# Zero products in the pauses of the first groups, last-group weights spread by selecting products, and a one-instruction residual sum, in an audio tower kernel

## The reference, cut to what matters

```python
h = tok(x)                                   # 92 patches of 16 x 32 -> 128 features
h = h + attn(layernorm(h))                   # 8 heads of 64; softmax, heads mixed 8x8, norm over heads, times v
h = h + ffn(layernorm(h))
# ffn, for each token t (T = 64 * 92):
scores = softmax(xf @ gate_w.T); topk_w, topk_i = top_k(scores, 2); topk_w /= topk_w.sum(-1)
combine[t, topk_i] = topk_w                  # T x 8, two entries per row
eo = relu(xf @ w1[e] + b1[e]) @ w2[e] + b2[e]     # eight experts
y = sum_e combine[:, e] * eo[e];  out = y + relu(xf @ sw1 + sb1) @ sw2 + sb2
```

## Time and profile before

| | |
|---|---|
| median of 3 runs | 630.79 us (629.08 to 631.88) |
| the profiled execution | 634.0 us, of it a span of 632.2 us |
| PE busy | 604.8 us, 96% of the span |
| PEld, DVE, ACT, POOL busy | 527.6, 435.9, 406.5, 369.5 us |
| chain that ended last | PE 89%, DVE 3%, ACT 2%, POOL 2%, DMA 2%, issue 1% |
| granted TensorE clock | mean 0.973 of full speed |

### The profile page before, as it was taken

The page is one execution under the profiler, slowest core; times in us unless marked ns, Lnnn a source line. Parts: engine busy times, 40 slices in busy tenths (PEclk is TensorE's granted clock), DMA queues, the critical chain, the costliest instruction groups (busy, mean ns, idle before and its releaser), DMA issues.

```text
span 632.2 us, 17001 instructions
## 1 busy us (share of the span) xinstructions
PE 604.8 (96%) x6275; PEld 527.6 (83%) x6275; DVE 435.9 (69%) x1322; ACT 406.5 (64%) x1346; POOL 369.5 (58%) x545
## 2 busy tenths in 40 slices
PE   8887889999999999999999999999999999998895
PEld 7767789898989989898989888898988888887773
DVE  4453647778677777778777767777687767776543
ACT  3476657686867767676867667676857767676110
POOL 2754538585766748575756748575756747546100
PEclk9987869999999999999999999999999999999897
DMA  6000030120303030120302030120303020201112
GB/s 233 25 3 26 1 98 26 38 98 10 126 2 109 27 110 26 49 87 14 121 2 111 25 111 25 59 78 14 123 2 121 16 109 3 85 25 42 70 30 91
DMA packets 15459, 37.43 MB, mean 59 GB/s; under 512 B 1808, under 2 KB 4240, under 8 KB 15376
## 3 DMA queue, kind: packets, MB, share of 16 engines
q1 hardware_dynamic: 15376, 36.34, 16.9%
HBM read 33.13 MB, written 3.20 MB: 57 GB/s over the span
## 4 chain that ended last, share of the span: by engine, by line
PE 89%; DVE 3%; ACT 2%; POOL 2%; DMA 2%; issue 1%; SPq 0%; DVEq 0%; POOLq 0%; ACTq 0%
PE ps_fill L413 16%; PE ps_fill L414 14%; PE ps_fill L415 13%; PE ps_mix L641 12%; PE ps_dots L629 11%; PE ps_fill L777 7%; PE ps_av L649 7%; PE ps_fill L569 5%; PE ps_fill L769 2%; PE ps_fill L751 1%; DMA spread<-weights 1%; PE ps_fill L752 1%; PE ps_fill L741 1%; POOL sum L1226 1%; ACT sq L810 1%
## 5 line engine op out<-in xcount | busy, mean ns | idle before, releaser
L802 ACT ACTIVATE ex<-ps_dots,negmax 128x92 f32<-128x92 f32 x384 | 123.9, 334 | 31.3 <-DVE negmax L1069 31.2
L1226 POOL TENSOR_TENSOR sum<-sq 92x384 f32<-92x384 f32 x64 | 64.1, 1002 | 73.7 <-ACT sq L810 73.6
L1220 POOL TENSOR_TENSOR probs<-ex,rinv 128x552 f32<-128x552 f32 x64 | 71.1, 1112 | 57.9 <-DVE rinv L1075 57.9
L1166 DVE SCALAR_TENSOR_TENSOR act<-ps_fill,b_neg,spread 128x368 f32<-128x368 f32 x123 | 68.3, 594 | 28.4 <-PE ps_fill L415 21.7
L641 PEld LDWEIGHTS ps_mix<-mixk,probs 64*92 64x92 f32 x1536 | 69.5, 161 | 18.2 <-issue 10.6
L641 PE MATMUL ps_mix<-mixk,probs 64*92 64x64 f32 x1536 | 78.3, 250 | 3.1 <-DVE aT L1085 2.7
L629 PE MATMUL ps_dots<-xT,yT 128*64 128x92 f32 x1536 | 76.8, 250 | 4.0 <-ACT ex L802 4.0
L629 PEld LDWEIGHTS ps_dots<-xT,yT 128*64 128x64 f32 x1536 | 65.0, 139 | 15.5 <-ACT ex L802 8.3
L802 ACT ACTIVATION_READ_ACCUMULATOR ex<-ps_dots,negmax 128x1 f32 x384 | 77.7, 202 | 0.0
L1085 DVE TENSOR_TENSOR aT<-ps_mix,arstd 92x384 f32<-92x384 f32 x128 | 64.3, 542 | 7.2 <-ACT arstd L820 7.2
L810 ACT ACTIVATE sq<-ps_mix 92x768 f32<-92x768 f32 x64 | 51.6, 806 | 13.2 <-PE ps_mix L641 12.2
(11 more groups left out here) (190 smaller groups left out, 1524.0 us busy)
## 6 DMA issues: line engine op xcount, KB each, us to landing
spread<-weights SPq DMA_DIRECT2D x64, 368.0 KB, 5.3
xin<-in_x SPq DMA_DIRECT2D x16, 372.0 KB, 3.0
out<-fT SPq DMA_DIRECT2D x16, 184.0 KB, 1.9
act<-w_raw SPq DMA_DIRECT2D x1, 576.0 KB, 6.5
w_sb<-w_raw SPq DMA_DIRECT2D x1, 576.0 KB, 7.2
qkv<-qk_raw SPq DMA_DIRECT2D x1, 512.0 KB, 5.1
spread<-tok_raw SPq DMA_DIRECT2D x1, 256.0 KB, 3.8
spread<-wv_raw SPq DMA_DIRECT2D x1, 256.0 KB, 5.3
```

The costliest lines, as they stand in the source:

```text
L802: last = act.activation(ex[:, s % 2, c, :], ps_dots[:, c // HALF, o:o + N], ACT.Exp, bias=negmax[:, c:c + 1], accum_out=sums[:, s % 2, c:c ...
L1166: dve.scalar_tensor_tensor(out=act1[:, e, :], in0=ps[:, 0:W], scalar=b1_neg[:, e:e + 1], in1=spread[:, e, :], op0=ALU.max, op1=ALU.mult).t ...
L1220: pool.tensor_tensor(probs[:, s % 2, :, :], ex[:, s % 2, :, :], rinv[:, s % 2, :].unsqueeze(2).broadcast_to([128, CHUNKS, N]), ALU.mult).t ...
L1226: pool.tensor_tensor(sum4[:, :, :, :], sq[:, :, 0:4, :], sq[:, :, 4:8, :], ALU.add)\
```

## The change

**Still products.** `STILL` lists four places: before `dots 2` and `mix 2` of iteration 0 (4 and 9 products), before `dots 1` and `CT` of iteration 1 (17 and 23). There `still_products` waits until a shared bank is free and issues that many 128 x 368 products of the zero columns of `act1_split[0]` into it; the next user of the bank overwrites them. `ORDER_1` is the same list as `STEPS` and serves only the counting of bank uses. `FILL_BUSY`, empty, goes.

**Selecting products.** POOL builds `shares` in `prepG` (iteration 0): for each expert a 128 x 128 matrix with ones in rows e and 32 + e. All eight first products of the last group move to iteration 16, behind `RT` (`T0` to `T7`, ahead of `YF` and `CT`), in five PSUM places used in turn; ACT empties them as relu into `spread`. In iteration 17, once `combT` is there, `S0` to `S7` multiply `shares[e]` with `combT`, which gives expert e's weight on all partitions in PSUM, and DVE makes `act1 = (spread - b1) * ps`. The store and loads of the last group's weights (lines 891, 548, 552) go.

**Residual.** `shift` adds the bias to hT on POOL (one instruction for two), and `OP` is one DVE instruction of 368 columns for four.

```diff
@@ -95,6 +95,8 @@
 WIDE = tuple(f"T{e}" for e in range(E))
+SHARES = tuple(f"S{e}" for e in range(E))
+PLACES = 5
@@ -112,7 +114,7 @@
              (LAST - 2, "TX2"): 15, (LAST - 2, "RT"): 6}
-FILL_BUSY = {}
+STILL = {(0, ("dots", 2)): (4, "Y7"), (0, ("mix", 2)): (9, "Y7"), (1, ("dots", 1)): (17, "OP"), (1, "CT"): (23, "Y1")}
@@ -138,6 +140,15 @@
+ORDER_1 = [('mix', 0), ('sq', 0), ('dots', 0), ('max', 0), 'XE', ('av', 0), 'Z0', 'XO', ('exa', 0), 'Z2', ('rstd', 0), 'Z1',
...
+ ('ev', 3)]
@@ -147,14 +158,17 @@
  [('mix', 0), ('sq', 0), ('av', 0), ('ev', 0), 'Z0', ('rstd', 0), ('scale', 0), 'Z5', 'Z1', 'Z8', ('av', 1),
-  ('ev', 1), 'Z4', 'Z6', 'OP', 'Z2', 'TH2', 'Z7', 'NH2', 'Z3', 'TX2', 'RT', 'R2', 'R3', 'YF', 'CT', 'hold'],
- ['Z8', 'Z3', 'T6', 'Z0', 'Z1', 'T5', 'T2', 'T7', 'T4', 'YF']]
+  ('ev', 1), 'Z4', 'Z6', 'OP', 'Z2', 'TH2', 'Z7', 'NH2', 'Z3', 'TX2', 'RT', 'T0', 'T1', 'R2', 'T2', 'T3', 'T4', 'T5',
+  'T6', 'T7', 'R3', 'YF', 'hold', 'CT'],
+ ['Z8', 'S0', 'S1', 'S2', 'S3', 'S4', 'S5', 'S6', 'S7', 'YF']]
...
         return ORDER_0
+    if isinstance(G, int) and G == 1:
+        return ORDER_1
@@ -213,6 +227,10 @@
         filled_then = [other for other in ORDER_0[:ORDER_0.index(step)] if present(other, G)] + SETUP
+        return more + sum(BANK.get(other) == BANK[step] for other in filled_then)
+    if isinstance(G, int) and G == 1:
+        filled_then = [other for other in ORDER_0 if present(other, 0)] + SETUP
+        filled_then += [other for other in ORDER_1[:ORDER_1.index(step)] if present(other, 1)]
@@ -329,6 +346,7 @@
         flat = sb("flat", [E, W])
+        shares = sb("shares", [128, E, 128], F32R)
@@ -494,8 +514,10 @@
-            n = [other for other in order(LAST - 1) if other in WIDE].index(step)
-            return [ps_dots[:, 0, :], ps_dots[:, 1, :], ps_mix[:, 0, :], ps_mix[:, 1, :], ps_av[:, :]][n], n + 1
+            steps = order(LAST - 2) + order(LAST - 1)
+            n = [other for other in steps if other in WIDE + SHARES].index(step)
+            places = [ps_dots[:, 0, :], ps_dots[:, 1, :], ps_mix[:, 0, :], ps_mix[:, 1, :], ps_av[:, :]]
+            return places[n % PLACES], n + 1
@@ -542,7 +564,7 @@
                     load(G + 2)
-                if step == "CT":
+                if step == "CT" and exists(G + LAG[step] + 1, NG):
@@ -614,6 +636,14 @@
+            def still_products(step, G):
+                count, free = STILL[G, step]
+                wait_free(pe, free, G)
+                columns = act1_split[0][:, 0:4, :].rearrange("p e w -> p (e w)")
+                for _ in range(count):
+                    pe.matmul(bank(free)[:, 0:W], columns[:, 0:128], columns[:, 0:W], start=True, stop=True)
@@ -655,6 +685,8 @@
                 keep_busy(step, G)
+                if (G, step) in STILL:
+                    still_products(step, G)
@@ -672,7 +704,19 @@
                         pe.wait_ge(oT_ready, B)
+                        wait_emptied(pe, "TX2", G)
+                    at_least(pe, wide_emptied, n - PLACES)
                     products(to[:, 0:W], [w[:, int(step[1]), :] for w in w1_split], [m[:, 0:W] for m in x2T])\
+                        .then_inc(wide_filled, 1)
+                    return
+                if step in SHARES:
+                    to, n = wide(step)
+                    if n == E + 1:
+                        pe.wait_ge(shares_ready, 1)
+                        wait_emptied(pe, "CT", G - 1)
+                    pe.wait_ge(wide_emptied, min(n - PLACES, E))
+                    at_least(pe, wide_scaled, n - PLACES - E)
+                    pe.matmul(to[:, 0:W], shares[:, int(step[1]), :], combT[:, :], start=True, stop=True)\
@@ -693,11 +737,6 @@
                     pe.wait_ge(oT_ready, SLOTS * g + SLOTS)
-                if FILL_BUSY.get(step, 0) and 0 <= g and G < LAST - 2:
-                    wait_free(pe, step, G)
-                    columns = w1_split[0][:, 0:4, :].rearrange("p e w -> p (e w)")
-                    for _ in range(FILL_BUSY[step]):
-                        pe.matmul(bank(step)[:, 0:W], columns[:, 0:128], columns[:, 0:W], start=True, stop=True)
@@ -759,10 +798,10 @@
                     if direct(G):
-                        experts = [other for other in order(G) if other in EXPERTS + WIDE + (f"Z{E}",)]
+                        experts = [other for other in order(G) if other in EXPERTS + SHARES + (f"Z{E}",)]
                         for other in experts:
-                            if other in WIDE:
-                                pe.wait_ge(wide_emptied, wide(other)[1])
+                            if other in SHARES:
+                                pe.wait_ge(wide_scaled, wide(other)[1] - E)
@@ -852,6 +891,13 @@
                 if step in WIDE:
+                    e = int(step[1])
+                    ps, n = wide(step)
+                    wait_emptied(act, f"Z{e}", G)
+                    act.wait_ge(wide_filled, n)
+                    act.activation(spread[:, e, :], ps[:, 0:W], ACT.Relu, bias=vecT[:, e:e + 1]).then_inc(wide_emptied, 1)
+                    return
+                if step in SHARES:
@@ -888,7 +934,8 @@
                     wait_filled(act, step, G)
-                    act.activation(flat[:, :], ps[0:E, 0:W], ACT.Copy).then_inc(weights_flat, 1)
+                    if exists(g + 1, NG):
+                        act.activation(flat[:, :], ps[0:E, 0:W], ACT.Copy).then_inc(weights_flat, 1)
@@ -1117,12 +1164,14 @@
                 if step in WIDE:
+                    return
+                if step in SHARES:
...
                     ps, n = wide(step)
-                    dve.wait_ge(weights_spread[e // 2], 16 * NG)
+                    dve.wait_ge(wide_emptied, wide(f"T{e}")[1])
                     dve.wait_ge(wide_filled, n)
-                    dve.scalar_tensor_tensor(out=act1[:, e, :], in0=ps[:, 0:W], scalar=b1_neg[:, e:e + 1],
-                                             in1=spread[:, e, :], op0=ALU.max, op1=ALU.mult).then_inc(wide_emptied, 1)
+                    dve.scalar_tensor_tensor(out=act1[:, e, :], in0=spread[:, e, :], scalar=b1_neg[:, e:e + 1],
+                                             in1=ps[:, 0:W], op0=ALU.add, op1=ALU.mult).then_inc(wide_scaled, 1)
@@ -1134,11 +1183,8 @@
                     wait_filled(dve, step, G)
-                    for s in range(SLOTS):
-                        last = dve.scalar_tensor_tensor(out=h2T[:, s, :], in0=ps[:, N * s:N * s + N],
-                                                        scalar=bias_old[:, s:s + 1], in1=hT_old[:, s, :],
-                                                        op0=ALU.add, op1=ALU.add)
-                    last.then_inc(emptied[BANK[step]], 1)
+                    dve.tensor_tensor(h2T[:, :, :], ps[:, 0:W].rearrange("p (s n) -> p s n", n=N), hT_old[:, :, :],
+                                      ALU.add).then_inc(emptied[BANK[step]], 1)
@@ -1208,6 +1254,9 @@
                     halve(w2_split, w2_sb[:, 0:2 * len(UNITS), :], 2)
+                    pool.wait_ge(table_loaded, 16)
+                    high, low = [ident[:, r:r + E].unsqueeze(2).broadcast_to([128, E, 128]) for r in (0, COPY)]
+                    pool.tensor_tensor(shares[:, :, :], high, low, ALU.add).then_inc(shares_ready, 1)
@@ -1269,8 +1318,8 @@
                     wait_read(pool, G, [("OP", 0), ("TK", 1), ("BS", 1)])
-                    pool.tensor_tensor(bias_old[:, :], bias[:, :], ones[:, :], ALU.mult)
-                    pool.tensor_copy(hT_old[:, :, :], hT[:, :, :]).then_inc(shifted, 1)
+                    pool.tensor_tensor(hT_old[:, :, :], hT[:, :, :], bias[:, :].unsqueeze(2).broadcast_to([128, SLOTS, N]),
+                                       ALU.add).then_inc(shifted, 1)
...
```

More of the change, by code:

```diff
@@ L123, in present @@
 def present(step, G):
-    if step in WIDE:
+    if step in WIDE + SHARES:
         return True
@@ L140 @@
  'V0', 'Y1', ('ev', 3)]
+ORDER_1 = [('mix', 0), ('sq', 0), ('dots', 0), ('max', 0), 'XE', ('av', 0), 'Z0', 'XO', ('exa', 0), 'Z2', ('rstd', 0), 'Z1',
+ ('scale', 0), ('exb', 0), ('inv', 0), ('ev', 0), 'H0', 'Z8', 'Z3', 'Z6', ('dots', 1), ('max', 1), ('av', 1),
+ ('mix', 1), ('ev', 1), 'H1', ('exa', 1), 'Z5', 'Z7', 'OP', ('sq', 1), 'Z4', ('exb', 1), ('rstd', 1), ('dots', 2),
+ 'shift', ('max', 2), ('inv', 1), 'TH2', ('exa', 2), 'TK', ('exb', 2), 'V3', ('scale', 1), ('mix', 2), 'NH2',
[4 rows of a table added]
 ORDERS_END = [[('mix', 0), ('dots', 0), ('sq', 0), ('max', 0), ('exa', 0), 'Z3', 'Z0', ('exb', 0), ('rstd', 0), ('av', 0), 'Z5',
@@ L297, in audio_tower @@
         bias = sb("bias", [128, SLOTS])
-        bias_old = sb("bias_old", [128, SLOTS])
         yT = sb("yT", [128, SLOTS, 2 * CHUNKS, HEADS, IR])
@@ L407, in audio_tower @@
         wide_emptied = sem("wide_emptied")
+        wide_scaled = sem("wide_scaled")
+        shares_ready = sem("shares_ready")
         def products(out, stationary, moving, start=True, stop=True):
@@ L1159, in do @@
                     e = int(step[1])
```

(2 more changed lines are left out.)

## The result

The changed kernel takes 621.64 us (median of 4 runs, 621.51 to 621.80); the kernel before, run beside it, 631.34 (4 runs, 629.08 to 632.14). The ratio is 0.9852, 95% interval 0.9825 to 0.9879. It is faster by 1.5%; 620.9 was forecast.

A forecast was written before the change was run, and what follows sets the result against it. PE bounds full groups; only half-clock stretches in the head and the end could move. 7.6 - 0.55 + 4.5 = 11.5 us off the profiled 634.0 gives 622.5, with half the median gap 620.9; range 617.0 to 626.5.

The forecast's parts named there:

- The likeliest case: Whole kernel: clock stays up in the head and at the new end, 620.9 us; chance 0.46.
- First stretch: Head, behind the 2.01 us pause: 3.42 us at half clock return to full clock, gain 0.8 us.
- Second stretch: Iteration 1, `dots 1` to `dots 2`: 9.18 us at 0.51 clock, gain 2.5 us, limited by ACT's exponentials.
- Third stretch: Behind the 4.20 us pause, up to iteration 2's first `mix`: 11.81 us at 0.60 clock, gain 4.3 us.
- Building `shares`: Iteration 0, POOL: one 2.35 us instruction delays `probs` of sequence 0, cost 0.55 us, between 0 and 0.9.
- Residual: Iteration 16, `TH2` waits for DVE's residual sum: gain 0.3 us, between 0 and 0.6; nothing in full groups.
- The end: Iterations 16 and 17: no weights DMA, final sum at full clock; gain 4.2 us, 4.5 with the residual.
- rival (a): New end: the clock falls in PE's thin work before the last `YF`, 623.8 us; chance 0.24.
- Rival (b): Head: a half-clock stretch stays or arises, costing 2.5 to 4.3 us, about 624.4 us; chance 0.17.
- Halving it: From profiled execution to median: half of the 3.2 us gap taken off, 622.5 to 620.9 us.
- (c): Head: products of zeros do not hold the clock outside the setup, no gain there, 628.5 us; chance 0.08.
- (d): Head: clock already low when still products start, each takes double, 639.9 or 638.3 us; chance 0.03.

The follow-up runs named there:

- `ek_no13`: `early_keep` without the first two sets of still products (4 and 9), the 17 and 23 kept; 618.69 us.
- `ek_oldres`: `early_keep` with the residual sum as before the change, four DVE instructions, bias and hT copied by POOL; 618.99 us.
- `head_keep`: Kernel before the change plus the still products and 18 more keep-busy products in iterations 15 and 16, with the old end and residual; 621.54 us.
- `early_keep`: Changed kernel with `shares` built ahead of the setup and 18 more keep-busy products in iterations 15 and 16; 618.23 us, ratio 0.9787.
- `head_only`: Kernel before the change with the 53 still products and nothing else; 624.70 us, ratio 0.9912.
- `ct_first`: `early_keep` with the last group's `CT` taken ahead of most of group 14's final sum, which is split around `S0` to `S4`; 616.23 us, ratio 0.9764.
- `keep_end`: Changed kernel with 8 more keep-busy products before av 3 of iteration 15 and 10 before av 1 of iteration 16; 618.98 us.
- `no_still`: Changed kernel with the table of still products empty, the rest kept; 629.62 us, ratio 0.9976.
- `shares_early`: Changed kernel with POOL's instruction that builds `shares` moved from iteration 0 to POOL's start, ahead of the setup; 619.99 us.
- experiment 1: `head_only` and `no_still`, beside the kernel before; its line through 33 runs of that kernel gives 0.39 us per us at half clock.
- `ek_data`: `early_keep` with the still products reading the experts' split weights in place of zeros; 618.16 us.
- `ek_double`: `early_keep` with twice the still products, 8, 18, 34 and 46; 625.69 us.

## Why the prediction was right

The likeliest case came true: the clock stays up in the head and at the new end, and the time is faster by 1.5%. That the total is only 0.7 us off is in part luck, since errors of 1.6 us and less, up and down, offset each other. Term by term, in profiled time:

**First stretch**, 0.8: the trace gave 0.9; in the medians `ek_no13` shows 0.5, not separable from nothing.

**Second stretch**, 2.5: this step was mis-sized; it gave 3.9. I took the full group's 6.60 us as what ACT's exponentials allow. The trace of before says otherwise: PE is busy for all of these 6.60 us, and the last of the exponentials is read out at 281.42, 1.04 us ahead of `dots 2`.

```profile
275.86:282.46 6.60, 6.60 (x87) 6.19 (x89) 4.31 (x11) 5.08 (x18) 6.17 (x6) 1.00 0.20 59
```
```profile
281.20 0.22 ACT L802 ACTIVATION_READ_ACCUMULATOR ex<-ps_dots,negmax 128x1 f32 x1
```

So the 6.60 were PE's own work: 21 products behind `mix 1`, where iteration 1 has 12. Nine fewer at 0.17 us leave about 5.1, close to the 5.26 measured. In the trace after, the last of the exponentials issued since `dots 1` starts at 61.73 and is read out by 62.16, 4.98 us after `dots 1`, while PE is busy until 62.44: PE sets the time here, and the bound I had set aside (4.5 for PE alone) was the nearer one.

```profile
61.94 0.22 ACT L841 ACTIVATION_READ_ACCUMULATOR ex<-ps_dots,negmax 128x1 f32 x1
```

**Third stretch**, 4.3: it gave 4.4.

**Building `shares`**, cost 0.55: mis-sized; it cost 1.1. Two errors. The instruction took 1.90 us and not 2.35, at 1.86 ns a column with both operands broadcast, where `probs` with one takes 2.0; and the path was not POOL's queue but DVE's. I had looked at the subtraction L987 as the instruction that might be locked out. It was the casts ahead of it, which I had not considered, that stood still. The figure of 1.2 by the rule of the Trainium skill's page "SBUF — State Buffer", which I had left out of the sum, was the nearer one, though it had the lock on another instruction and a POOL instruction of 2.35 us.

**Residual**, 0.3: by the traces 0.4 (`ek_oldres`); the medians don't separate it from nothing.

**The end**, 4.2, or 4.5 with the residual: 4.8 in the profile. The steps held one by one: `CT` behind `YF`, `CT` to `YF` 4.20 us for 4.1 forecast, `YF` to fT 6.03 for 6.15, no weights DMA, and clock 1.00 throughout, which is against rival (a). Of the 4.8, 3.0 are the final sum's clock (9.01 us before, 6.03 after), and 1.8 the shorter way from `h2T` to `YF` (23.10 and 21.30 us). In medians it is 3.3 (`head_keep` against `early_keep`), since how long the old end stays at half clock differs from run to run, and the profiled execution of before is at the long side: from `YF` to fT the same sum takes 9.01 us there, 8.52 in `head_keep` and 7.64 in `head_only`. And three of `head_keep`'s four runs took 621.44 to 621.63 us at a mean clock of 0.997, or 3.7 us at half clock in all, the profiled one 622.62 at 0.995. The delay of `CT` by 3.75 us, which I booked as the price of the new order, was avoidable: `ct_first` takes 2.0 us of it back.

**What no term held.** A second stretch at half clock arises in iterations 15 and 16 beside the one that was there. Rival (b) has such a stretch arise, but in the head; these iterations are in no term and no rival: `h2T` comes 0.8 us later than the head's gain would have it. `keep_end` removes both stretches, for 2.7 us. The same eight products take 2.63 and 2.54 us in the traces of `head_only` and `no_still`, and 1.60 in those of before and `shares_early`, all behind the same idle time of 1.51 us. So no one half of the change is needed for this drop, and one trace of each kernel can't tell a kernel from an execution: why it comes in some and not in others is not settled.

**From sum to median.** 11.5 us forecast against 12.5 found, as +1.6 for the head, -0.55 for `shares`, -0.8 for iterations 15 and 16, +0.3 for the end and residual, and +0.4 of setup that no edit touches. The 3.2 us gap between the profiled execution and the median was not the profile's own cost, as I half assumed: at its mean clock of 0.973 the line of experiment 1 gives 633.3 us of the 634.0. It was half-clock time, which the change removes, and cannot be saved twice. So the sum counts from 634.0 and nothing more comes off: 634.0 - 12.5 = 621.5, where the median is 621.6. Halving it took 1.6 off, which offset the 1.0 that my sum was short: luck, not method.

**The rivals.** (c), zeros hold no clock, falls by `head_only` and `ek_data`. (d), doubled products in front of ready work, does not occur, as the clock was still up where each set began; `ek_double` shows its price even at full clock: 7.5 us.

## What to carry to other kernels

Behind pauses of 2 to 4 us on TensorE the work of this kernel ran at half clock for longer than the pause lasted in most executions, so look at the granted clock of the windows behind each pause, not at the pause; cheap products into a free bank, counted from the pause's length and one product's pace, buy it back, and too many cost most of their own time (7.5 of 9.4 us here). When an edit moves TensorE's work in time, look at every thin stretch again, also far from the edit. Before an instruction on GpSimd is put beside VectorE's work, look at all that VectorE does in that time, copies and casts between SBUF tiles too; before work elsewhere is taken as a bound on a wait, look which engine was busy to its end; and when the profiled execution is slower than the median, compare their mean clocks before deciding what the gap is.

## What the hardware showed that I had not expected

- Three VectorE casts of 8 x 128 from SBUF to SBUF took 2.23 us beside one GpSimd instruction of 1.90 us, and 0.68 without it.
- The time of this kernel follows the clock granted in each execution: 0.39 us per us at half clock, over 33 runs from 625.5 to 634.5 us. With a mean clock of 0.999 or 1.000 in all, four runs of a kernel still differ by 0.13 (`keep_end`) to 1.00 us (`early_keep`).
- Products of zeros and of weights hold TensorE's clock alike (618.23 and 618.16 us). Half as many hold it in some executions only (619.59 to 624.18 us): a stretch of 3.00 us with 1.43 us of work had 1.00 behind it, one of 5.00 us with 2.62 of work had 0.62, and in the kernel after one of 4.00 us with 2.20 had 0.57.
